# A fused attention and routed-expert layer: value products two slots later, one row-sum product group per pair, one score product for both heads in narrow slots

## The reference, cut to what matters

```python
q = einsum('bld,dhk->blhk', x, Wq)
latent = einsum('bld,dc->blc', x, Wkv_down)
k = einsum('blc,chk->blhk', latent, Wk_up);  v = einsum('blc,chk->blhk', latent, Wv_up)
attn = softmax(where(causal, q @ k / 8, -inf))
x = layernorm(x + einsum('bqhd,hdo->bqo', attn @ v, Wout))
# then a router over 32 experts (top 1, capacity 320), gate/up/down products of 256x256,
x = layernorm(x + gate * expert(x))
```

## Time and profile before

| | us |
|---|---|
| median of 3 runs (2668.49 to 2669.42) | 2668.54 |
| profiled execution, its own time | 2669.0 |
| its span, first to last instruction | 2666.9 |
| attention part, first to last slot, about | 53 to 2329 |
| mean granted clock of TensorE | 0.968 |

### The profile page before, as it was taken

How to read it: one execution, slowest core, us unless ns; L and a number is a source line. 1 busy time by engine, 2 the same in 40 slices (tenths; PEclk the granted TensorE clock), 3 DMA queues, 4 the chain that set the end, 5 groups by cost and what they waited for, 6 DMA issues and landing times.

```text
span 2666.9 us, 35643 instructions
## 1 busy us (share of the span) xinstructions
PE 2466.4 (92%) x12040; PEld 1578.6 (59%) x12040; DVE 1532.1 (57%) x4298; ACT 994.5 (37%) x1480; POOL 1674.7 (63%) x1623
## 2 busy tenths in 40 slices
PE   6999999999999999999999999999999999959995
PEld 5555665556655665566555655566556655646663
DVE  3666556665666556655666476656665666235453
ACT  3344424442444334433444244433443344212222
POOL 0677656865687657766686468665876678523343
PEclk7999999999999999999999999999999999969998
DMA  2122100200011001100020002000110011233552
GB/s 82 57 66 71 37 10 16 68 17 13 15 52 31 13 13 40 40 17 13 17 66 18 9 17 64 17 17 9 44 41 13 17 32 33 64 106 126 167 169 67
DMA packets 96804, 118.88 MB, mean 45 GB/s; under 512 B 12288, under 2 KB 75782, under 8 KB 96624
## 3 DMA queue, kind: packets, MB, share of 16 engines
q1 hardware_dynamic: 89712, 99.98, 13.4%
q0 software_dynamic: 6912, 16.64, 1.8%
HBM read 46.91 MB, written 37.90 MB: 32 GB/s over the span
## 4 chain that ended last, share of the span: by engine, by line
PE 62%; POOL 17%; issue 11%; DVE 6%; ACT 2%; DMA 1%; POOLq 0%; SPq 0%; ACTq 0%; DVEq 0%
PE value_ps L692 14%; POOL sums L475 10%; PE turned_ps L669 9%; PE row_ps L645 7%; PE turned_ps L672 7%; PE misc_ps L593 6%; PE misc_ps L711 4%; PE turned_ps L857 4%; PE misc_ps L702 4%; POOL probs L451 2%; POOL slots_x L508 2%; DVE masked_row L1078 1%; ACT probs L928 1%; PE misc_ps L876 1%; PE value_ps L876 1%
## 5 line engine op out<-in xcount | busy, mean ns | idle before, releaser
L928 ACT ACTIVATE probs<-turned_ps 128x1024 f32<-128x1024 f32 (+3 forms) x768 | 616.9, 811 | 961.2 <-PE turned_ps L672 953.1
L475 POOL TENSOR_TENSOR sums<-sums,probs 128x1024 f32<-128x1024 f32 (+3 forms) x512 | 830.6, 1622 | 23.1 <-ACT probs L928 14.7
L1078 DVE CUSTOM_DVE_ANT_0 masked_row<-row_ps,future 128x384 bf16<-128x384 f32 (+3 forms) x1024 | 464.4, 489 | 406.2 <-PE row_ps L645 405.1
L692 PE MATMUL value_ps<-probs,lat_keys 128*64 128x512 f32 (+3 forms) x3072 | 607.5, 508 | 44.8 <-POOL probs L451 41.2
L669 PE MATMUL turned_ps<-q_hl,lat_hi 128*128 128x512 f32 (+3 forms) x1536 | 570.3, 379 | 1.5 <-ACT fold_v L974 1.5
L672 PE MATMUL turned_ps<-q_max,lat_lo 65*128 65x512 f32 (+3 forms) x1536 | 528.4, 352 | 2.6 <-DMA q_max<-max_rows 2.6
L451 POOL TENSOR_SCALAR_AFFINE_SELECT probs<-probs 128x256 f32<-128x256 f32 x512 | 210.3, 411 | 500.3 <-ACT probs L928 499.6
L645 PE MATMUL row_ps<-lat_hi,q_hl 128*128 128x512 f32 (+3 forms) x1536 | 452.8, 366 | 14.3 <-DVE unit_max L1078 7.3
L471 POOL TENSOR_TENSOR sums<-probs 128x768 f32<-128x768 f32 (+1 forms) x128 | 268.5, 2097 | 233.0 <-ACT probs L928 233.0
L669 PEld LDWEIGHTS turned_ps<-q_hl,lat_hi 128*128 128x128 f32 x1536 | 294.2, 192 | 197.3 <-issue 149.0
L692 PEld LDWEIGHTS value_ps<-probs,lat_keys 128*64 128x64 f32 x3072 | 180.7, 137 | 348.5 <-issue 222.4
(11 more groups left out here) (187 smaller groups left out, 2317.4 us busy)
## 6 DMA issues: line engine op xcount, KB each, us to landing
q_max<-q_hl SPq DMA_DIRECT2D x256, 128.0 KB
slots_x<-zero_rows SPq DMA_DIRECT2D x8, 1290.0 KB, 6.4
ex_x<-slots_x SPq DMA_DIRECT2D x64, 129.0 KB, 3.5
x_in<-in_L_attn_x_bld SPq DMA_DIRECT2D x8, 1024.0 KB, 6.0
layer_out<-x_in SPq DMA_DIRECT2D x8, 1024.0 KB, 5.0
ex_w<-in_L_ffn_w_gate SPq DMA_DIRECT2D x32, 256.0 KB, 3.7
ex_w<-in_L_ffn_w_up SPq DMA_DIRECT2D x32, 256.0 KB, 3.8
ex_w<-in_L_ffn_w_down SPq DMA_DIRECT2D x32, 256.0 KB, 4.0
```

The costliest lines, as they stand in the source:

```text
L475: nc.gpsimd.tensor_tensor(sums[c][:, :, q0:BANK], sums[c][:, :, q0:BANK], now[:, :, q0:BANK], ALU.add).then_inc(added, 1)
L692: mm = nc.tensor.matmul(value_ps[h * LD:(h + 1) * LD, q0:BANK], lat_keys[b % 2][:, j, :], probs[:, n % NPROBS, h, q0:BANK], start=(j == 0) ...
L928: nc.scalar.activation(probs[:, n % NPROBS, :, q0:BANK], turned_ps[n % 2][:, :, q0:BANK], ACT.Exp).then_inc(exp_done, 1)
L1078: nc.vector.tensor_tensor_reduce(masked_row[n % 2][:, 0:width], row_ps[n % 2][:, 0:width], future[:, BANK - width:], scale=-1.0, scalar=-M ...
```

## The change

What it does, in seven parts. (1) `LAG` = 2: in even slots PE computes the values of the slots four and three before it, instead of two and one before; ACT's `copy_heads` moves two slots later with it (slots 2 and 6), and after the last slot four slots' values are left instead of two. (2) Row sums: one `sums` stage per pair, in slot 4 of the next pair, instead of two; four products with a 32-column matrix of ones, for two heads and two halves, each in its own 32 columns of the array, into one bank. The tile of half 0 is doubled. DVE transposes the bank once (in slot 5, one slot after PE's stage; before it was the same slot), and inverts it in two steps in slots 6 and 8, each with two new copies of 32 partitions x 16 (so that both halves' results stand on all 64 partitions of a head). (3) Slots of 256 and 128 queries (2, 3, 10, 11): both heads' scores in one product of twice the width, in one bank: two products instead of four. (4) `maxT` of the next pair's half 0 goes from `EARLY` in slot 4, ahead of the row scores, to `LATE` in slot 6. (5) `divide` on POOL goes from slots 0 and 6 to slot 7 (half 0) and slot 0 two pairs on (half 1); `roots`, `variance`, `normalise`, the gate's exponentials, `proj`, `x1T`, `logits` and `pos` are placed later, `q` of two pairs in slot 7 instead of 8. (6) The last pair's eight projections go from slots 1 to 10 into slots 9 to 11. (7) Memory: `wkv2` and the zero rows share tiles with others.

```diff
+    LAG = 2
-        ones_f = sb("ones_f", [P, LD], F32, attn)
+        ones_f = sb("ones_f", [P, 32], F32, attn)
-        sums = [sb(f"sums{c}", [P, 2, BANK], F32, attn) for c in range(2)]
+        half_sums = [sb(f"half_sums{i}", [P, 2, BANK], F32, attn) for i in range(3)]
+        sums_of = lambda gp, c: half_sums[2 if c else gp % 2]
...
-                EARLY[gp, 4] = [("maxT", gp + 1, 0)]
+                late[6].append(("maxT", gp + 1, 0))
             if gp:
-                late[4].append(("sums", gp - 1, 1))
-            late[6].append(("sums", gp, 0))
+                late[4].append(("sums", gp - 1))
             if gp + 2 < PAIRS:
-                late[9 if p == NPAIR - 2 else 8].append(("q", gp + 2, 0))
+                late[9 if p == NPAIR - 2 else 7 if b and p < 2 else 8].append(("q", gp + 2, 0))
             if b and p == 0:
-                for i, t in enumerate((3, 5, 7, 10, 11)):
+                for i, t in enumerate((9, 10, 11)):
                     late[t].append(("proj", b - 1, i))
             if b and p == 1:
-                for i, t in enumerate((3, 5, 7)):
-                    late[t].append(("proj", b - 1, 5 + i))
-                for kd in range(KD):
-                    late[10 + kd].append(("x1T", b - 1, 0, kd))
+                for i, t in enumerate((3, 5, 9, 10, 11)):
+                    late[t].append(("proj", b - 1, 3 + i))
             if b and p == 2:
-                for kd in range(KD):
-                    late[3 + 2 * kd].append(("x1T", b - 1, 1, kd))
-                late[7].append(("logits", b - 1))
+                for use, t in zip([(hf, kd) for hf in range(2) for kd in range(KD)], (3, 5, 7, 10)):
+                    late[t].append(("x1T", b - 1, *use))
+                late[11].append(("logits", b - 1))
             if b and p == 3:
-                late[3].append(("pos", b - 1))
+                late[7].append(("pos", b - 1))
...
-        for t, i in zip((1, 2, 3, 5, 7, 8, 9, 10), range(NT)):
+        for t, i in zip((9, 9, 10, 10, 11, 11, 11, 11), range(NT)):
             LATE[PAIRS - 1, t].append(("proj", LAST, i))
...
+        in_one_bank = lambda t: 2 * (BANK - first_query(t)) <= BANK
+        def scores_of(n):
+            q0 = first_query(n % NSLOT)
+            if in_one_bank(n % NSLOT):
+                return turned_ps[n % 2][:, 0, 0:2 * (BANK - q0)].rearrange("p (h q) -> p h q", h=2)
+            return turned_ps[n % 2][:, :, q0:BANK]
...
-                    if gp and t == 0:
+                    if gp >= 2 and t == 0:
+                        divide(gp - 2, 1)
+                    if gp and t == 7:
                         divide(gp - 1, 0)
-                    if gp and t == 6:
+                    if gp == PAIRS - 1 and t == 9:
                         divide(gp - 1, 1)
-                    if b and (p, t) in ((1, 0), (2, 0)):
+                    if b and (p, t) in ((1, 8), (2, 2)):
                         roots(b - 1, p - 1)
...
+                if in_one_bank(t):
+                    nc.tensor.matmul(scores_of(n), lat_hi[b % 2][:, keys], q_hl[gp % 2][:, :, cols], start=True, stop=False)
+                    nc.tensor.matmul(scores_of(n), lat_lo[b % 2][:, keys], q_max[:, c, :, q0:BANK], start=False, stop=True
+                                     ).then_inc(turned_full, 1)
+                    return
...
-            def total(gp, c):
-                use = ("sums", gp, c)
+            def total(gp):
+                use = ("sums", gp)
                 bank = take(use)
-                pe.wait_ge(added, gp * NADD + (HPB if c == 0 else NADD))
+                pe.wait_ge(added, (gp + 1) * NADD)
                 for h in range(2):
-                    mm = nc.tensor.matmul(bank[h * LD:(h + 1) * LD, :], ones_f[:, :], sums[c][:, h, :], start=True, stop=True)
+                    for c in range(2):
+                        k = 2 * h + c
+                        mm = nc.tensor.matmul(bank[k * 32:(k + 1) * 32, :], ones_f[:, :], sums_of(gp, c)[:, h, :],
+                                              start=True, stop=True)
...
-                    if t % VALUES == 0 and gp + t:
-                        values(gp * NSLOT + t - VALUES)
+                    if t % VALUES == LAG % VALUES and gp * NSLOT + t >= VALUES + LAG:
+                        values(gp * NSLOT + t - LAG - VALUES)
...
-                    if t == 0 and gp:
+                    if t == LAG and gp:
                         copy_heads(gp - 1, 1)
-                    if t == 4:
+                    if t == 4 + LAG:
                         copy_heads(gp, 0)
...
-                nc.vector.reciprocal(rinv[:, :], sums_cols[:, :].rearrange("p (n q) -> p n q", q=32)[:, :, 0]
+                nc.vector.reciprocal(rinv[:, c, :], sums_cols[:, :].rearrange("p (n q) -> p n q", q=32)[:, :, 0]
                                      ).then_inc(inverse_done, 1)
-                dve.wait_ge(inverse_done, n + 1)
+                dve.wait_ge(inverse_done, 3 * n + 1)
+                for h in range(2):
+                    src, dst = (64 * h + 32 * k for k in (c, 1 - c))
+                    nc.vector.tensor_copy(rinv[dst:dst + 32, c, :], rinv[src:src + 32, c, :]).then_inc(inverse_done, 1)
+                dve.wait_ge(inverse_done, 3 * n + 3)
...
                             if use[0] == "sums":
-                                invert_rows(*use[1:])
+                                invert(*use[1:])
+                    if gp and t in (6, 8):
+                        invert_rows(gp - 1, t // 8)
```

More of the change, by code:

```diff
@@ L245, in build_layer @@
         EARLY, LATE = {}, {}
-        last_sums = ("sums", PAIRS - 1, 1)
+        last_sums = ("sums", PAIRS - 1)
         for gp in range(PAIRS):
@@ L463, in add_probs @@
                 if c == 0 and j == 0:
-                    if gp:
-                        pool.wait_ge(misc_full, MISC["sums", gp - 1, 0] + 1)
-                    nc.gpsimd.tensor_copy(sums[0][:, :, 0:P], now[:, :, 0:P]).then_inc(added, 1)
+                    if gp >= 2:
+                        pool.wait_ge(misc_full, MISC["sums", gp - 2] + 1)
+                    nc.gpsimd.tensor_copy(sums_of(gp, 0)[:, :, 0:P], now[:, :, 0:P]).then_inc(added, 1)
                 elif j == 1:
                     if c == 1 and gp:
-                        pool.wait_ge(misc_full, MISC["sums", gp - 1, 1] + 1)
+                        pool.wait_ge(misc_full, MISC["sums", gp - 1] + 1)
                     before = probs[:, (n - 1) % NPROBS]
-                    nc.gpsimd.tensor_tensor(sums[c][:, :, q0:BANK], before[:, :, q0:BANK], now[:, :, q0:BANK], ALU.add
+                    nc.gpsimd.tensor_tensor(sums_of(gp, c)[:, :, q0:BANK], before[:, :, q0:BANK], now[:, :, q0:BANK], ALU.add
                                             ).then_inc(added, 1)
@@ L474, in add_probs @@
                     pool.wait_ge(added, gp * NADD + ADDS_OF[t] - 1)
-                    nc.gpsimd.tensor_tensor(sums[c][:, :, q0:BANK], sums[c][:, :, q0:BANK], now[:, :, q0:BANK], ALU.add
-                                            ).then_inc(added, 1)
+                    total = sums_of(gp, c)[:, :, q0:BANK]
+                    nc.gpsimd.tensor_tensor(total, total, now[:, :, q0:BANK], ALU.add).then_inc(added, 1)
             def divide(gp, c):
@@ L989, in _ @@
                         pass_alone(b - 1, t)
-                    if b and (p, t) == (2, 10):
+                    if b and (p, t) == (3, 4):
                         gate_exponentials(b - 1)
@@ L1076, in row_max @@
                 dve.wait_ge(rows_full, n + 1)
+                row = row_ps[n % 2]
                 if k * BANK + width == (i + 1) * P:
-                    nc.vector.tensor_tensor_reduce(masked_row[n % 2][:, 0:width], row_ps[n % 2][:, 0:width], future[:, BANK - width:],
+                    nc.vector.tensor_tensor_reduce(masked_row[n % 2][:, 0:width], row[:, 0:width], future[:, BANK - width:],
                                                    scale=-1.0, scalar=-MASKED, op0=ALU.add, op1=ALU.min, accum_out=dst
@@ L1081, in row_max @@
                 else:
-                    nc.vector.tensor_reduce(dst, row_ps[n % 2][:, 0:width], AX.X, ALU.max, negate=True
+                    nc.vector.tensor_reduce(dst, row[:, 0:width], AX.X, ALU.max, negate=True
                                             ).then_inc(max_done, 1)
@@ L1260, in _ @@
                 if use[0] == "sums":
-                    invert_rows(*use[1:])
+                    for c in range(2):
+                        invert_rows(PAIRS - 1, c)
                 if use[0] == "rest" and use[2] == HPB - 1:
```

38 lines of the change are left out of this document (20 added, 18 removed).

## The result

The changed kernel takes 2728.43 us (median of 4 runs, 2722.4 to 2733.28) against 2668.51 us for the kernel before beside it (4 runs): ratio 1.0227, 95% interval 1.0208 to 1.0247. It is **slower by 2.3%**, where 2.7% faster was forecast. The profiled execution's own time is 2731.29 us, its span 2729.2 us.

A forecast was written before the change was run, and what follows sets the result against it. PE, busy 92% of the span, was taken to bound the kernel. From 2669 us, -68 over seven batches, -1 for batch 0 and -4 for the ending gave 2596 us; own range 2572 to 2618, 8 in 10 within 2555 to 2652.

The forecast's parts named there:

- The copies: In `invert_rows`, slots 6 to 8: two new DVE copies of 32 x 16, 0.15 us each (bounds 0.08 and 0.28).
- slot 5 term: In slot 5 a stage waits for the sums' transpose, which DVE runs one slot later: 1.6 us in all.
- The clock: In pair 2's sum: one added term of 1.5 us for a low clock.
- The value lag: PE's 95.4 us wait on POOL's mask: 75 saved, 0.4 us a pair and 7.1 us in each of seven batches.
- The router's steps: In pair 3: position and router steps on DVE add 1.1 us, giving 30.3 us.
- The sums stage: Slot 4: new stage streams 0.86 us plus 0.2 for the column switch, replacing two of 0.96; net 0.75 saved a pair.
- Rival B: In the sums stage, four column groups run two at a time: +55 us, 2651 us; chance 0.16.
- C: Rival: the sums stage's four column groups don't overlap, so it takes 3.44 us: +165 us, 2761 us; chance 0.05.
- Narrow slots: Two products instead of four save 0.22 us in slots 3 and 11 each, nothing in 2 and 10: 0.45 a pair.
- DVE's pace: In plain pairs PE waits for DVE, giving back 1.7 of 2.0 us gained: 29.2 us against 29.48.
- rival A: DVE doesn't pace: 1.7 us more gained in about 40 plain-like pairs, 68 us, 2528 us; chance 0.13.
- The ending: Last pair's projections moved to its last three slots: -6 us; then a chain of inverses and `divide`: +2.

The follow-up runs named there:

- run 3: Changed kernel with reciprocals for the copies, copy_max and other late stages ahead of `invert_rows`, and sums transposed by DVE in slot 4: 2592.06 us, ratio 0.9707.
- run 1: Changed kernel with DVE's two 32x16 copies per inverse replaced by reciprocals that read the other half's partitions: 2649.99 us, ratio 0.9928.
- run 10: Kernel before plus a block after its last expert timing ten DVE operations against POOL's additions and with POOL idle; one execution, POOL's additions 1.53 us each.
- Run 2: Changed kernel with copy_max and the other late stages ahead of `invert_rows`, the copies kept: 2674.97 us, ratio 1.0018.
- run 4: Kernel before with the value lag alone (values and copy_heads two slots later): 2666.99 us, ratio 0.9986.
- run 6: The kernel of run 3 with no value lag (`LAG = 0`): 2599.47 us, ratio 0.9725.
- Run 12: The kernel of run 3 with the router's position step of pair 3 in slot 3 instead of slot 7: 2577.27 us, ratio 0.9652.
- run 7: The kernel of run 3 without the single product in narrow slots (one product per head again): 2603.51 us, ratio 0.9747.

## Why the prediction was wrong

The time is 132 us over the forecast of 2596. Three edits to what DVE does and when, and none to PE's program, take 136 us of it back (run 3); the steps that had these wrong come first.

**The copies.** The step that failed is "two new copies of 32 x 16 which no row shows (bounds 0.08 and 0.28 each ...; I take 0.15)". Measured: 0.62 us on average, 158.4 - 256 x 0.165 = 116 us of holding, up to 2.15 us for one of them; run 1 prices it at 78 us. I bounded it by short DVE rows of the kernel before. The longer of them, the 0.28 of L1093 in rows 5, ran inside an addition of POOL but reads PSUM, and run 10 shows that a copy from there is not held (0.68 us with POOL adding and with POOL idle). So the upper bound was no bound: that is the length of POOL's longest instruction, 2.4 us. The trace of the kernel before did show a hold. The router's L1178, with two inputs in SBUF, takes 0.42 us in six of its eight records and 2.53 in two; one of these (DVE, then POOL):

```profile
1001.21 2.53 DVE L1178 TENSOR_TENSOR onehot<-expert_m,rt 128x256 bf16<-128x256 f32 x1
...
1001.11 2.35 POOL L475 TENSOR_TENSOR sums<-sums,probs 128x1024 f32<-128x1024 f32 x1
```

In a plain pair the hold is small (29.25 us against 28.85 in run 1), since there DVE meets the last 0.6 us of the addition. Taken over to the copies, the two long records of L1178, 2.53 us against 0.42, would have put the worst case in the range.

**misc_ps in slot 7.** The prediction put down stalls "in slot 3" and "in slot 5" and wrote "then copy_max" behind the 1.4 us of `invert_rows`, but gave slot 7 no term, though four pairs of a batch have a stage there and pair 3 the position step. The waits there are 63 us over the kernel. Run 2 gains 53 us, though not beside run 1's 78: most of the wait was for the copies. Of the slot 5 term of 1.6 us, run 3 shows 1.2 to 1.3 us, and that it was avoidable.

**The clock.** The sum had it as one term, 1.5 us in pair 2, and none for the stops. No run shows that term: the 0.50 of the earlier trace rows lies in pair 2 of the kernel before; in the changed kernel the granted clock is 0.50 from 740.8 to 744.2, behind the logits of batch 2 but in pair 3, and in run 3 pair 2 takes 33.8 us at 1.00 in six of seven batches, 34.65 at 0.97 in batch 1. The clock has two levels in these profiles: cut into stretches of 1 us, the changed kernel shows 1.00 in 2414 of 2660 and 0.50 in 173, and only 73, where it changes, lie between. An estimate from the profiled executions: at a mean granted clock of 0.957 the changed kernel spent 2 x 0.043 x 2729 = 235 us at the lower level, and run 3, at 0.965, 182 us; half of the difference, at most some 27 of the 136 us, is the clock's share.

**The value lag.** "Of the 95.4 us I take 75": runs 4 and 6 show 0 to 7. The wait did go, and DVE's pace in slot 4 took its place: a plain pair does not gain the 0.4 us but is longer with the lag by 0.41 (run 4 against the kernel before) and 0.34 (run 3 against run 6). The 7.1 us a batch were counted in full.

**The router's steps.** They were priced at 1.1 us in pair 3, as if their place did not matter; in the changed kernel the same hold hits one of them (L1231, 2.08 us). Run 12 against run 3: 15 us for the whole kernel.

**The sums stage.** By its own terms the new stage is 0.86 + 0.2 us and the two old ones 1.92, which is 0.86 saved and not 0.75: the 0.1 behind a stage was counted twice. Measured: 1.92 - 1.00 = 0.92.

**Right.** Rival B and C are out: the four column groups run at once, 1.00 us for the stage. Of the 0.2 charged for the switch from 64 to 32 columns little is seen: the stage is 1.00 us long from start to start, where 0.86 was streaming, and the old stage had 0.10 there too. Narrow slots: 0.19 us in slot 3 (forecast 0.22), and by run 7 0.22 a pair net of what DVE's pace takes back (forecast 0.45 gross). DVE's pace as the new bound (rival A out): plain pair 29.25 against 29.2. Four pairs of run 3 are close to the forecast ones: 38.2 against 38.0 (pair 0), 44.8 against 45.8 (pair 1), 35.5 against 37.2 (pair 6), 29.3 against 30.2 (pair 7). Pair 2 is shorter, 33.8 against 36.1, with a granted clock of 1.00 in batch 2 where 1.5 us were charged for a low one; pair 3 is longer, 34.1 to 36.6 against 30.3. That run 3 lies within 4 us of 2596 is partly luck: it lacks the stall in slot 5 that was charged, and the lag gave less than was counted.

**The ending** was forecast at -6 + 2. From the start of the last pair to the end of the kernel it is +5: 397.0 us against 391.9. The last pair up to its sums takes 51.9 us (2332.26 to 2384.15) against 54.1, since the eight projections, now back to back, wait for DVE to free the bank between each other; from the sums on PE waits for `divide` as forecast, but longer:

```profile
2374.75 3.29 PE L733 MATMUL misc_ps<-fold_v,headsT 128*128 128x256 f32 x14 [0.59 <-DVE x L1163]
...
2384.15 1.07 PE L723 MATMUL row_ps<-half_sums,ones_f 128*32 128x512 f32 x8
2388.98 0.74 PE L743 MATMUL row_ps<-fold_v,headsT 128*128 128x256 f32 x2 [3.77 <-POOL headsT L495]
```

4.83 us from the sums to the first projection behind them, 1.22 before. Another 3.7 us lie behind that projection and are not explained.
